# Graph transformer layer on one core: the last layer's side work placed anew, and expert results scattered to node rows instead of gathered at the end

## The reference

```python
def _rgcn_layer(x, W, root, bias, src, dst, seg):          # three of these, relu, relu, sigmoid
    agg = segment_sum(x[src], seg, num_segments=N_REL * N_NODES).reshape(N_REL, N_NODES, -1)
    return einsum('rnd,rde->ne', agg, W) + x @ root + bias

def _L0_ffn_ref(x, Wr, br, ln_g, ln_b, W1, b1, W2, b2):    # a mixture of 8 experts, top 2
    probs = softmax(xt @ Wr + br);  top_p, top_idx = top_k(probs, 2)
    weights = top_p / top_p.sum(axis=-1, keepdims=True)
    xe = layernorm(xt) * ln_g[e] + ln_b[e]
    y = gelu(xe @ W1[e] + b1[e]) @ W2[e] + b2[e]           # hidden width 1024
    return (weights[:, :, None] * y[top_idx]).sum(axis=1)

xn = _layernorm(x)
x = x + gnn(xn) + linear_attention(xn[None])[0]
x = x + _L0_ffn_ref(_layernorm(x)[None], ...)[0]
return x
```

## Time and profile before

| | |
|---|---|
| median of 3 runs | 3810.72 us (3805.47 to 3815.09) |
| the profiled execution | 3800.47 us, its span 3798.7 us |
| PE busy, of the span | 2900.7 us (76%) |
| POOL busy | 2397.5 us (63%), 2396 gathers of edge rows |
| DVE, ACT busy | 1179.5 us (31%), 447.0 us (12%) |
| mean granted TensorE clock | 0.841 of full speed |

### The profile page before, as it was taken

The page is one execution under the profiler, slowest core; times in us unless marked ns, Lnnn a source line. Parts: engine busy times, 40 slices in busy tenths (PEclk is TensorE's granted clock), DMA queues, the critical chain, the costliest instruction groups (busy, mean ns, idle before and its releaser), DMA issues.

```text
span 3798.7 us, 51045 instructions
## 1 busy us (share of the span) xinstructions
PE 2900.7 (76%) x16228; PEld 2552.1 (67%) x16228; DVE 1179.5 (31%) x2813; ACT 447.0 (12%) x1220; POOL 2397.5 (63%) x2537
## 2 busy tenths in 40 slices
PE   3878777877778888888888778787767777777791
PEld 3776766776666676677666567776666666667791
DVE  5232223222232223222322233333332333333312
ACT  1000000000000000000000010122121211212230
POOL 5777777777757777777776677755445554543005
PEclk9888888898888778877878777798888888888896
DMA  7444444444443333333333333555444454544653
GB/s 175 133 146 132 133 146 133 132 136 143 133 131 110 108 108 109 108 108 108 109 107 100 116 105 105 161 167 160 143 139 159 142 160 137 156 147 133 216 187 112
DMA packets 272287, 511.76 MB, mean 135 GB/s; under 512 B 60237, under 2 KB 177119, under 8 KB 272032
## 3 DMA queue, kind: packets, MB, share of 16 engines
q0 software_dynamic: 120864, 330.20, 29.8%
q1 hardware_dynamic: 150000, 178.85, 14.8%
q10 hardware_dynamic: 1296, 1.24, 0.1%
HBM read 453.68 MB, written 56.42 MB: 134 GB/s over the span
## 4 chain that ended last, share of the span: by engine, by line
POOL 45%; PE 25%; issue 20%; DVE 4%; DVEq 2%; DMA 1%; ACT 1%; ACTq 1%; POOLq 0%; SPq 0%
POOL arena L590 44%; PE bank L1584 6%; PE bank L1530 4%; PE bank L1599 3%; PE bank L1643 3%; PE bank L1639 2%; PE bank L1777 2%; PE bank L1787 2%; POOL arena L655 1%; ACT arena L777 1%; PE bank L1523 1%; DVE arena L1193 1%; DVEq L1228 1%; DMA arena<-rows_dram,arena 0%; PE bank L1521 0%
## 5 line engine op out<-in xcount | busy, mean ns | idle before, releaser
L590 POOL DMA_INDIRECT arena<-rows_dram,arena x2396 | 2268.8, 947 | 906.7 <-issue 751.9
L1639 PE MATMUL bank<-arena 128*128 128x128 f32 x4836 | 1082.2, 331 | 436.0 <-DMA arena<-rows_dram,arena 374.9
L1639 PEld LDWEIGHTS bank<-arena 128*128 128x128 f32 x4836 | 855.3, 223 | 636.9 <-DMA arena<-rows_dram,arena 469.3
L1278 DVE TENSOR_TENSOR arena<-arena,bank 128x256 f32 x807 | 340.4, 422 | 2226.3 <-PE bank L1643 2123.2
L1643 PE MATMUL bank<-arena 128*128 128x128 f32 x4836 | 798.7, 310 | 0.0
L1643 PEld LDWEIGHTS bank<-arena 128*128 128x128 f32 x4836 | 732.1, 226 | 0.0
L1530 PE MATMUL bank<-arena 128*128 128x256 f32 x2400 | 600.3, 390 | 0.0
L1530 PEld LDWEIGHTS bank<-arena 128*128 128x128 f32 x2400 | 445.4, 198 | 49.2 <-issue 0.5
L1584 PE MATMUL bank<-arena 128*128 128x128 f32 x1152 | 220.2, 370 | 255.7 <-DVE arena L1152 171.0
L1584 PEld LDWEIGHTS bank<-arena 128*128 128x128 f32 x1152 | 207.7, 279 | 264.9 <-issue 264.9
L1211 DVE TENSOR_TENSOR arena<-bank,arena 128x1408 f32<-128x1408 f32 x222 | 355.3, 1603 | 13.0 <-issue 13.0
(11 more groups left out here) (204 smaller groups left out, 1373.0 us busy)
## 6 DMA issues: line engine op xcount, KB each, us to landing
arena<-in_L_ffn_W_dram SPq DMA_DIRECT2D x112, 512.0 KB, 4.3
arena<-in_L_ffn_W_dram SPq DMA_DIRECT2D x44, 1024.0 KB, 6.2
arena<-rows_dram,arena POOLq DMA_INDIRECT x2418, 2.8
xs_dram<-zrow SPq DMA_DIRECT2D x25, 1152.0 KB, 5.6
arena<-xs_dram SPq DMA_DIRECT2D x56, 128.0 KB, 2.1
xs_dram<-arena SPq DMA_DIRECT2D x56, 128.0 KB, 2.7
rows_dram<-arena SPq DMA_DIRECT2D x50, 128.0 KB
arena<-in_L_gnn_weights_dram SPq DMA_DIRECT2D x6, 1024.0 KB, 8.8
```

The source lines that it names most:

```text
L590: nc.gpsimd.indirect_dma_start(out=gath[:, slot, :], out_offset=None, in_=rows_dram[l], in_offset=bass.IndirectOffsetOnAxis(ap=idx_ring[:, ...
L1278: nc.vector.tensor_tensor(acc, acc, bank[EDGE_BANKS[q % 3]][:, 0:KD * WC].rearrange("p (k r n) -> p k r n", k=KD, r=REL), ALU.add).then_in ...
L1639: nc.tensor.matmul(bank[EDGE_BANKS[q % 3]][:, 0:WC], gath[:, slot, 0:P], onehot[:, slot, :], start=first, stop=last)
```

## The change

**The last layer's places.** The table of places gets new numbers. DVE's are now counted in groups q, and an item placed at group q comes before that group's add, where it came after the group's add before. An expert slot's turn moves ahead of its hidden halves, and the two hidden halves move apart. Router, `route` and `dealt` move from the next span to the end of the same one and the start of the next. The router's results and the ranks share the turning bank, and `early_o` has one half of a PSUM bank for each of the two slots. The 11 window positions of a span are read by DVE four at a time.

**The results.** Rows of `xs_dram` are 272 floats wide; the 257th is the row in a new table `ys_dram` to which the result belongs (node row for choice 0, node row + 3200 for choice 1; a fill row for padding). DVE writes two copies of each normalised row, one per choice, each with its number. In the tail POOL scatters each slot's result to `ys_dram` (20 of them), and the 36 early results are reloaded by SP, three per tail slot through four buffers, and scattered as well. After the tail, SP reads the two tables with 10 plain DMAs of up to 640 KB and two of 53 KB; the 50 gathers are gone.

```diff
-STAGE, LAST_STAGE, POST, TURN, BACK = 4, 11, 17, 23, 26
+STAGE, LAST_STAGE, POST, TURN, BACK = 4, 11, 14, 23, 26
-MIX_ROW, MIX, MIX_ADD = 24, 27, 29
-X2, YN, XN2, DEV1, DEV2, YBACK, YTURN, ROUTE = 20, 23, 26, 21, 24, 28, 27, 1
+MIX_ROW, MIX, MIX_ADD = 24, 27, 10
+X2, YN, XN2, DEV1, DEV2, YBACK, YTURN, ROUTE = 5, 6, 7, 19, 19, 29, 27, 30
...
-RT, RT_MM, RT_POS = 5, 7, 11
-PICK, LAST_PICK = (14, 17), (13, 13)
-PLACE = (dict(turn=0, scale=2, h0=4, h1=8, out=16, bias=20), dict(turn=17, scale=20, h0=22, h1=25, out=29, bias=32))
-LAST_PLACE = (dict(turn=0, scale=2, h0=4, h1=8, out=12, bias=13), dict(turn=-1, scale=-1, h0=-1, h1=-1, out=-1, bias=-1))
+RT, RT_MM, RT_POS = 10, 2, 3
+PICK, LAST_PICK = (3, 4), (4, 4)
+LOADS = 4
+PLACE = (dict(turn=2, scale=0, h0=8, h1=15, out=22, bias=8), dict(turn=19, scale=6, h0=22, h1=29, out=32, bias=11))
+LAST_PLACE = (dict(turn=2, scale=0, h0=8, h1=11, out=13, bias=5), dict(turn=-1, scale=-1, h0=-1, h1=-1, out=-1, bias=-1))
...
+            def reload(j):
+                b = j % RELOAD_BUFS
+                sp.wait_ge(s_ye[j % 2], 16 * (j // 2 + 1))
+                wait(sp, s_ysent[b], 16 * (j // RELOAD_BUFS))
+                t = sp.value_load(slot_t[0:1, bass.ds(j, 1)], min_val=0, max_val=EXP * NT - 1)
+                sp.dma_start(again[b], slot_rows(xs_dram, t)).then_inc(s_again[b], 16)
+
+            for s in range(TAIL):
+                if s + 2 < TAIL:
+                    sp.wait_ge(S["xs_back"], s + 1)
+                    load_rows(s + 2, s % 2)
                     sp.wait_ge(S["hid_mm"], 2 * s + 2)
-                    load_weights(s + 2, c)
...
+                    load_weights(s + 2, s % 2)
+                for j in range(RELOADS * s, min(RELOADS * (s + 1), EARLY)):
+                    reload(j)
...
-                    for j in range(TG):
-                        nc.gpsimd.indirect_dma_start(out=back[b][:, j, :], out_offset=None, in_=xs_dram,
-                                                     in_offset=bass.IndirectOffsetOnAxis(ap=pos[:, g * TG + j, c:c + 1], axis=0)).then_inc(s_back[b], 16)
+
+            def send(rows, at, signal):
+                nc.gpsimd.indirect_dma_start(out=ys_dram, out_offset=bass.IndirectOffsetOnAxis(ap=at, axis=0),
+                                             in_=rows, in_offset=None).then_inc(signal, 16)
+
+            for s in range(TAIL):
+                for j in range(RELOADS * s, min(RELOADS * (s + 1), EARLY)):
+                    b = j % RELOAD_BUFS
+                    pool.wait_ge(s_again[b], 16 * (j // RELOAD_BUFS + 1))
+                    send(again[b][:, 0:D], again[b][:, D:D + 1].bitcast(I32), s_ysent[b])
+                if s > 0:
+                    pool.wait_ge(s_ys[(s - 1) % 2], 16 * ((s - 1) // 2 + 1))
+                pool.wait_ge(S["out_back"], s + 1)
+                send(orow[s % 2], tail_rows[:, s:s + 1], s_ys[s % 2])
...
-                nc.vector.tensor_scalar(xn2[b], yrow, mv2[:, 0, 0:1],
-                                        rstd2[:, 0:1], ALU.subtract, ALU.mult).then_inc(S["xn2_made"], 1)
+                for c in range(TOPK):
+                    nc.vector.tensor_copy(xn2[b][c][:, D:D + 1].bitcast(I32), row_of[:, c, bass.ds(t, 1)])
+                    m = nc.vector.tensor_scalar(xn2[b][c][:, 0:D], yrow, mv2[:, 0, 0:1], rstd2[:, 0:1], ALU.subtract, ALU.mult)
+                m.then_inc(S["xn2_made"], 1)
...
                         for q in range(groups):
...
+                            if q % LOADS == 0:
+                                n = min(LOADS, groups - q)
+                                wins += nc.values_load_multi_w_load_instructions(
...
+                            beside(q)
```

More of the change, by code:

```diff
@@ L353, in places, with turned_ahead @@
             return LAST_PLACE if is_last(s) else PLACE
+        def turned_ahead(u):
+            return sum(at["turn"] < u for at in PLACE)
         def is_int(v, n):
@@ L1227, in span @@
                         groups = -(-tiles // GT)
[L1228 to L1234 removed]
+                        wins = []
```

227 lines of the change are left out of this document (110 added, 117 removed).

## The result

| | before | after |
|---|---|---|
| median of 4 runs | 3809.24 us | 3439.47 us (3438.18 to 3442.68) |
| the profiled execution | 3800.47 us | 3440.71 us, its span 3438.9 us |

The ratio is 0.9029, with a 95% interval of 0.9014 to 0.9045. The forecast was 3472 us, with a range of 3425 to 3600.

A forecast was written before the change was run, and what follows sets the result against it. POOL's gathers bound layers 0 and 1; in the last layer PE and DVE wait on each other. Span 3798.7 - 305 (last layer) - 37 (end) + 3 (tail) = 3459.7 us, plus 1.8 and 10.2: 3472 us, range 3425 to 3600.

The forecast's parts named there:

- Floor of the gathers: Last layer: undisturbed, 806 gathers at 1.252 us and 22 scatter pairs (57.2 us) put the last gather at 3170.7.
- 46 us per span: Last layer's spans on PE: 39.3 us of full-clock work, 3.5 of waits and 3.2 of half-clock loss.
- the whole 34 us that I had put behind POOL's floor: Last layer's end: at 46 us per span the last add comes at 3225, against 3191 with POOL as bound.
- The clock: PE in the last layer: half-clock loss shrinks from 7.0 to 3.2 us per span as waits go.
- the two rows that I had weighed: Clock evidence: spans 2 to 6 show 0.80 with hardly a wait; the tail shows 1.00 with PE never idle.
- the more work PE has, the higher the clock in every stage: Argument against the rival that the last layer's clock stays (3524 us, chance 0.22).
- Waits by place: PE's waits at each new place in the last layer: together 3.5 us per span, bounds 1 and 10.
- Seven tiles between the halves: Hidden halves in the last layer: the distance exceeds the 3 us gelu and its table need, so 0 us of wait.
- Tail: Slots after the last layer: reloads and scatters add 3 us in all, bounds 0 and 40.
- End: From the last bias to the last instruction: 40 us instead of 77.2, so 37 us less (32 to 42).
- The sum: Whole run: 3798.7 - 305 - 37 + 3 = 3459.7 us of span; with 1.8 outside and 10.2 to the median, 3472.
- Signs named beforehand: Profile marks of a right forecast: gather spacing, span time, hidden-line waits, clock, tail slots of 7.24 us, end of 38 to 42.

The follow-up runs named there:

- near: The changed kernel with each early slot's second hidden half nearer the first, and in a span's first slot the first half nearer its scaling: 3509.8 us, ratio 0.9220.
- twice: The changed kernel with the early slots' hidden matmuls computed a second time into the same bank: 3549.4 us on a chip as the first.
- half the work: The changed kernel without one of two contraction steps in early slots' hidden matmuls: 3441.5 us on a chip as the first, 4565.9 us on the second.
- the kernel with eleven reads: The changed kernel with all eleven window-position reads at a span's start instead of four: 4645.3 us, measured on the second chip alone.

## Why the prediction was right, and where its terms were not

**Floor of the gathers: right.** I had the last gather at 3170.7, and the last add at 3191 if POOL is the bound. The gather starts at 3173.8; the layer itself starts 3.3 us later (2107.64 against 2104.37). The last group is done at 3196.1, 5 us later than 3191.

**46 us per span: too much; this is the term that was mis-sized.** The full-clock work of 39.3 us was taken from durations of before, with 3.5 us of waits and 3.2 of half clock on top. Measured are 2.7 us of waits and 41.1 - 39.3 = 1.8 us that the clock took (0.96 granted): 43.8. Both terms had the right cause and too large a size, by 0.8 and 1.4 us, 2.2 together. That was enough to change which engine is the bound, and so the whole 34 us that I had put behind POOL's floor were not there. The last group is done at 3196.1 and not at 3225: 29 us, nearly all of what the forecast missed.

**The clock.** I chose between a stage at 0.80 with few waits and the tail at 1.00. That time is lost to the granted clock, two pieces of the kernel before show: behind a wait of 7.38 us sixteen hidden records took 3.76 us at a clock of 0.50 (at 2896.59), and with no wait just ahead of them 1.79 us at 1.00 (at 3325.99). What rows show now, in the full spans: PE idle for 29%, 13%, 7%, 5% of the time in before, near, after and twice, and a clock of 0.86, 0.93, 0.96, 0.98. In these spans the loss went with the waits. It does not hold everywhere. In the early spans of the last layer, which the changed kernel runs as before, PE has only short waits for gathers:

```profile
2200.00:2244.00 44.00, 38.40 (x184) 33.28 (x184) 17.18 (x46) 4.53 (x10) 33.22 (x35) 0.69 0.37 105
2244.00:2288.00 44.00, 36.11 (x184) 31.11 (x183) 16.45 (x45) 4.53 (x10) 33.33 (x36) 0.77 0.37 106
...
PE bank L1674 <- DMA arena<-rows_dram,arena: 14.4, 24, 1.8
```

The last line is of 2244 to 2376: 24 waits in 132 us, none over 1.8 us. PE is idle for 13% and 18% of the first two stretches, less than in the full spans of before, and yet the clock is 0.69 and 0.77 and not 0.86. The kernel with half the work points the same way: it has 33 waits for gathers of up to 3.0 us, the shortest hand-offs of the five, and a clock of 0.92. So neither of the two rows that I had weighed stands for every stage of this kernel, and the idle share alone does not tell the clock. What else sets it was not shown. Nor did the forecast's "the more work PE has, the higher the clock in every stage" fit: PE is busy for 80% of the first stage at 0.85 and for 71% of the third at 0.87.

**Waits by place.** "0 to 1 us" for the scalings came to 24.3 / 13.6 = 1.8 us per span; that wait is the largest that is left. Seven tiles between the halves were taken to hide gelu, and they do: waits of at most 1.1 us, and with three or four tiles between them of up to 4.0. The forecast counted the distance as one item among many. The run with the halves near shows that taking it back costs 68 us, since PE's slack is 0.2 us a span.

**Tail: inside the bounds, four times the value.** I took 3 us (0 to 40) and it is 12.2. I had named what costs it, weights issued behind the reloads of the slot before, each of which waits for a scatter. What I didn't do was count them: three reloads a slot through four buffers need a buffer back within 1.3 slots. The rate of the transfers was the other suspect; at 253 and 256 GB/s with and without the loss, nothing here shows it to be what cost time.

**End: right.** 37 us forecast, 37.7 measured. By parts: scatter and landing 3.7 us (3403.1 less 3399.4; I had 3.7 to 4), first tables 6.6 (7), combines 16.7 + 1.8 + 4.2 = 22.7 (22.5), last store 6.0 (6.3). It is closer than it looks: the 1.8 us are DVE waiting for the last table, which is issued only at 3418.72 and lands 9.50 us later. The chain that ended last runs through SP's issues and that landing, and not through the combines that the forecast summed:

```profile
3418.72 9.50 DMA arena<-ys_dram
...
3428.24 2.08 DVE xtok L1479 x5
```

**The sum.** 3459.7 us of span was forecast and 3438.9 came: 29.3 less in the last layer, 0.7 less at the end, 9.2 more in the tail. I then added 12 us for what lies around the span and for the profiled run's distance from the median; the changed kernel's median is 0.6 us above its profiled span. Correcting for a single execution that lay 10 us low carried an accident of that execution into the forecast.

**Signs named beforehand.** Gathers 1.25 us apart without a gap: yes. 44 to 47 us per span: 44.0. Waits of the hidden line for DVE under 5 us in two spans: 3.6. Clock over 0.92: 0.96. Slots of 7.24 us in the tail: no, while reloads run. 38 to 42 us at the end: 39.9.

## What to carry to other kernels

When two engines' chains come out within a few per cent of each other, put an edit on the distance between a producer and its consumer, and count a wait as slack only if it is for the engine that is the bound; the other waits belong to the chain itself. Before moving work to a queue that also carries the critical loads, divide its buffers by its rate and look who is queued behind the wait for a buffer. Spread background transfers over all of the stage that is to hide them.

## What was not expected of the hardware

The same kernel, two reloads per slot, in the same stretch of layer 0 on the second chip and on one as the first; columns as in the earlier trace rows:

```profile
800.00:1000.00 200.00, 117.88 (x658) 106.49 (x656) 43.97 (x65) 9.99 (x38) 115.85 (x123) 0.74 0.35 108
```

```profile
800.00:1000.00 200.00, 158.44 (x902) 137.52 (x901) 59.93 (x89) 14.01 (x53) 151.32 (x160) 0.88 0.46 139
```

A gather takes 0.94 or 0.95 us on either (115.85 / 123, 151.32 / 160), but on the second chip there are fewer: 33 of them take 53.7 us instead of 41.3. A piece of PE's timeline on the second chip shows a hole:

```profile
934.39 0.83 PE L1674 MATMUL bank<-arena 128*128 128x128 f32 x6
935.06 1.37 PE L1678 MATMUL bank<-arena 128*128 128x128 f32 x6
949.27 2.90 PE L1517 MATMUL bank<-arena 128*128 128x128 f32 x12 [12.84 <-issue]
```

PE does nothing for 12.84 us and waits for nothing that the profile shows. Near this hole DVE is idle for 10.75 us before its add at 945.25, and ACT for 19.33 us before its copy at 948.75; POOL goes on, one gather each 1.25 us. In that run PE has 105 stretches of over 4 us without work, 1057 us in sum, up to 25 us long, about one per span of 53.7 us in layer 0. They stand ahead of L1569 (27), L1674 (26), L1517 (20), L1634 (14) and others. For 43 of them, 363 us, the profile names no releaser; for the other 62 it names DVE, ACT or a DMA, so PE is not the only one that is late. On the other chip the same program has 6 such stretches, 71 us in sum (both worked out from all matmul records). The two profiles have the same 51466 instructions, and the tail, with 197.9 against 198.6 us, hardly differs.

What fills the holes isn't told by any row. The profile of the second chip also shows less of who waits for whom: it has no landing time for the gathers and for the 512 KB weight loads, where the other one has 2.8 and 4.6 us. So a missing releaser there does not show that there was none.

For the reading it matters twice. On a chip whose PE stands still, PE's chain becomes the bound, so that half of the hidden work is worth 83 us there and nothing on a chip as the first. And the change's ratio of 0.903 holds for chips without the holes; on the other one the kernel with eleven reads gives 0.951 (0.948 to 0.954).
